# A query bias row and nine gate rows computed by f16 products with the thin matrix standing, on one core

## The chip, the cores and the metric

One core of one Trainium2 chip runs the whole program. The metric is the device time of one execution in microseconds (us), median of several runs. The engines are called PE (TensorE), DVE (VectorE), ACT (ScalarE), POOL (GpSimd) and SP (the queue that issues most DMAs); PEld is PE's loading of the standing operand.

## The reference

x is 8 x 512 tokens of width 512, the context 8 x 120 rows of width 512. A cross-attention layer and an expert layer follow each other:

```
h  = layernorm(x)
kp = ctx @ Wk.T ;  vp = ctx @ Wv.T + bv ;  qp = h @ Wq.T + bq
x1 = x + (softmax(qp @ kp.T / sqrt(512)) @ vp) @ Wo.T + bo
z  = layernorm(x1)
e  = argmax(softmax(z @ Wg + bg))            # one of 8 experts for each token
out = x1 + gelu(z @ W1[e] + b1[e]) @ W2[e] + b2[e]
```

## The kernel before

The kernel has three stages. The first, the preparation, folds weights so that less is left for each token: `kq` is Wk.T @ Wq (key and query weights in one), `ov` is the product of the value and the output weights, and the keys of all eight batches (`J_KEYS`) and their values (`J_VAL`) are made from the context with these. The second stage takes 32 tiles of 128 tokens through attention, picks an expert for each token and writes the rows, sorted by expert, to memory. The third takes 39 tiles of sorted rows through the experts' two layers.

Precision is held by splitting an f32 matrix into a high and a low f16 half (scaled by `WSCALE` = 64) and adding three f16 products of halves; `PARTS` lists the three pairs. So one 512-column f32 result with an inner size of 512 costs four inner blocks x 3 = 12 matmuls. ACT writes the high half and DVE the low half of a result that is split again. ACT, DVE and POOL split the early experts' weights in the same way (`high`, `low`, `split`).

Every product of the preparation is a job with a number. Job n writes PSUM bank n % 8, PE counts finished jobs in `pre_mm`, and ACT and DVE count their copies in `pre_act` and `pre_dve`; `free(n)` makes PE wait until job n - 8 has been copied. The order on each engine is written out by hand and is strict. PE's order is: the products of `kq` (line 1391), the turning of twelve bias rows into columns (line 1399), the column sums of the gate weights (line 1404), the turning of the context (1414) and of Wo (1423), the eight key jobs (1450), the four `ov` jobs (1470), the value bias of the gate (1481, 1484), the value bias (1493), the key bias rows (1503), the eight value jobs (1515) with one turning (1524) among them, and then the token loop, which opens with the turning of x (line 1538).

Two thin results are made beside these. `J_U` is Wk.T @ bq, one number for each of 512 rows: while the second four key jobs run, after each group of three f16 products, `small` adds one f32 product with a 128 x 128 block of Wk standing and one column of the bias moving. `J_WOG` is made in the same places from Wo and the centred gate weights (9 columns). `J_WVG` is Wv times that result (9 columns), one small f32 product after each group of three of the four `ov` jobs. An f32 product is two PE instructions in the trace. Both thin results go to `row_weights` (128 x 4 x 10), are split (lines 850 and 1081) and stand in the key bias products of line 1503.

DVE's order in the preparation: the low halves of Wk and Wq (1036), of `kq` (1022), the copy of the bias columns (1043), the centred gate weights (1049), the split of the value bias (1051, 1053), the low halves of the context and of Wo (1022), the moments of all 32 tiles of x (1027, 1030), the low halves of `ov` (1022), the split of `row_weights` (1081), the copy of the gate's value bias (1085), and then the low halves of the experts' weights (1067) with the copies of the value bias (1091) and the values (1103) among them. SP loads x in groups into four buffers, each refilled when DVE's moments have read it; only behind the sixteen groups come the weights of experts 1 to 3 in its queue, and behind the last moments those of expert 4. The copy of the last value job on DVE also waits for nine pad transfers (`pad_out`), which POOL issues when expert 4 has landed.

Of the kernel before, what the change touches and what calls it, by code (L numbers as in the profile page):

```python
# [5 lines left out]
F16 = mybir.dt.float16  # L6
I32 = mybir.dt.int32
ALU = mybir.AluOpType
# [3 lines left out]
P = 128  # L12
# [128 lines left out]
def build(nc, x, ctx_in, Wk, Wv, bv, Wq, bq, Wo, bo, Wg, bg, W1, b1, W2, b2, out):  # L141
# [6 lines left out]
    with ctx:  # L148
# [22 lines left out]
        key_bias = split_area[0:1 + EM, :]  # L171
        b_stage = bias_area[0:BIAS_ROWS, 0:D]
# [20 lines left out]
        row_weights = sb("row_weights", [P, C, 1 + EM])  # L193
# [142 lines left out]
        rows_split = sem("row_weights_split_parts")  # L336
# [48 lines left out]
        NCONST = 20  # L385
# [23 lines left out]
        J_GSUM = job("dve")  # L409
        J_CTX = job("both", B)  # L410
        J_WOT = job("both", C)
        J_KEYS = job("act", 2 * C)
        J_U = job("act")
        J_WOG = job("act")
        J_OV = job("both", C)
        J_WVG = job("act")
        J_VGB = job("dve")
# [35 lines left out]
        def _(sp):  # L453
# [31 lines left out]
            sp.wait_ge(pre_mm, J_KQ + C)  # L485
# [125 lines left out]
        def _(pool):  # L611
# [10 lines left out]
            nc.gpsimd.memset(bias_rows, 0.0).then_inc(consts, 1)  # L622
            nc.gpsimd.iota(seen[:, 0, :], pattern=[[SPAN // P, E]], base=1, channel_multiplier=0,
# [175 lines left out]
        def _(act):  # L799
# [23 lines left out]
            for k in range(C):  # L823
                n = J_KQ + k
                copy(n, kq[:, 0, k, :], bank[n % 8][:, :], 1.0 / WSCALE)
            for b in range(B):
                n = J_CTX + b
                w = min(P, B * K - P * b)
                copy(n, ctxT[:, 0, :, P * b:P * b + w], bank[n % 8][:, 0:C * w].rearrange("p (c s) -> p c s", c=C))
# [10 lines left out]
            n = J_U  # L840
            copy(n, row_weights[:, :, 0], bank[n % 8][:, 0:C], SCALE)
            n = J_WOG
            copy(n, wo_gate[:, :, :], bank[n % 8][:, 0:C * EM].rearrange("p (c e) -> p c e", c=C))
            for k in range(C):
                n = J_OV + k
                copy(n, ov[:, 0, k, :], bank[n % 8][:, :], 1.0 / WSCALE)
            n = J_WVG
            copy(n, row_weights[:, :, 1:1 + EM], bank[n % 8][:, 0:C * EM].rearrange("p (c e) -> p c e", c=C), 1.0 / WSCALE)
            act.wait_ge(pre_act, copies("act", J_WVG))
            nc.scalar.activation(row_split[:, 0, :, :], row_weights[:, :, :], ACT.Copy, scale=WSCALE).then_inc(rows_split, 1)  # L850
# [155 lines left out]
        def _(dve):  # L1006
# [44 lines left out]
            nc.vector.tensor_scalar(bv_split[:, 0, :], bcol[:, C:2 * C], WSCALE, None, ALU.mult).then_inc(bv_parts, 1)  # L1051
            dve.wait_ge(bv_parts, 1)
# [22 lines left out]
            def ov_low(k):  # L1075
                low_part(J_OV + k, [ov[:, h, k, :] for h in range(2)], bank[(J_OV + k) % 8][:, :], 1.0 / WSCALE)

            for k in range(C):
                ov_low(k)
            dve.wait_ge(rows_split, 1)  # L1080
            nc.vector.scalar_tensor_tensor(row_split[:, 1, :, :], row_weights[:, :, :], WSCALE, row_split[:, 0, :, :],
                                           ALU.mult, ALU.subtract).then_inc(rows_split, 1)
# [288 lines left out]
        def _(pe):  # L1371
# [34 lines left out]

            for b in range(B):
                n = J_CTX + b
                free(n)
                if b in (0, 4, 7):  # L1410
                    pe.wait_ge(ctx_in_at[(0, 4, 7).index(b)], 16)
                w = min(P, B * K - P * b)
                for c in range(C):
                    last = nc.tensor.transpose(bank[n % 8][:, w * c:w * (c + 1)], ctx_nat[0:w, b, P * c:P * (c + 1)],
                                               ident[0:w, 0:w])
                last.then_inc(pre_mm, 1)
# [16 lines left out]
            bq_cols = [bcol[:, e:e + 1] for e in range(C)]  # L1433
# [3 lines left out]
            for h in range(2):  # L1437
                for b in range(4 * h, 4 * h + 4):
                    copied(pe, J_CTX + b)
                if h == 1:  # L1440
                    copied(pe, J_BIAS)
                    copied(pe, J_GSUM)
                    free(J_U)
                    free(J_WOG)
                for c in range(C):
                    n = J_KEYS + C * h + c
                    free(n)
                    for k in range(C):
                        for u, v in PARTS:
                            last = mm(bank[n % 8][:, 0:4 * K], kq[:, u, k, P * c:P * (c + 1)],  # L1450
                                      ctxT[:, v, k, 4 * K * h:4 * K * (h + 1)],
                                      start=(k == 0 and u + v == 0), stop=(k == C - 1 and u == 1))
                        if h == 1:
                            last_u = small(J_U, C * c + k, wk_sb, bq_cols, 1)
                            last_wog = small(J_WOG, C * c + k, wo_sb, wg_cols, EM)
                    last.then_inc(pre_mm, 1)
            last_u.then_inc(pre_mm, 1)
# [5 lines left out]
            free(J_WVG)  # L1463
            wo_cols = [wo_gate[:, e, :] for e in range(C)]
            for k in range(C):
                n = J_OV + k
                free(n)
                for e in range(C):
# [3 lines left out]
                    if k == 0 and e == 0:  # L1472
                        copied(pe, J_WOG)
                    last_wvg = small(J_WVG, C * k + e, wv_sb, wo_cols, EM)
                last.then_inc(pre_mm, 1)
            last_wvg.then_inc(pre_mm, 1)
# [20 lines left out]
            pe.wait_ge(rows_split, 2)  # L1497
# [10 lines left out]
            for k in range(C):  # L1508
                copied(pe, J_OV + k)
# [227 lines left out]
```

## Time and profile before

| | |
|---|---|
| median of 3 runs | 430.65 us (425.63, 430.65, 430.79) |
| profiled execution | 428.8 us, span 427.1 us |
| mean granted TensorE clock | 0.986 |
| busy in the span: PE, DVE, ACT, POOL | 394.9, 321.9, 250.7, 264.7 us |

The span runs from the first to the last instruction of the profiled execution; 1.7 us of its time lie outside. In timelines a row is start, length, engine, line and what was done, with the idle time before it and what ended that in brackets. An engine's busy time says how full it is on average and not what it holds up: that is read from the stretch of the preparation that the change touches.

### The profile page before, as it was taken

Reading aid. Unit: us, or ns where it says so; the run is one execution under the profiler, and the core shown is the slowest. Engines: PE = TensorE matmul, PEld = TensorE weight load, DVE = VectorE, ACT = ScalarE, POOL = GpSimd, SP = SyncE. Lnnn points to the kernel's source line nnn. Section 1 sums busy time; section 2 is a strip of 40 time slices with the busy share of each in tenths; the row PEclk is TensorE's granted clock in tenths of the full one; section 3 lists DMA queues with packets and bytes.
Section 4 is the critical chain, followed back from the end, with each engine's and each line's share of the span. In section 5 each row is a group of like instructions: output and inputs, shape, how many; then the busy total and the mean of one; then the engine's idle time right before and its main releaser. Section 6 shows DMA issues by size and latency. Waiting matters only on the chain.

```text
span 427.1 us, 8876 instructions
## 1 busy us (share of the span) xinstructions
PE 394.9 (92%) x2097; PEld 219.9 (51%) x2097; DVE 321.9 (75%) x658; ACT 250.7 (59%) x571; POOL 264.7 (62%) x338
## 2 busy tenths in 40 slices
PE   7999999979999998997877999999999999999970
PEld 4657774648777676663333444444444444444430
DVE  3499849993678888888687777878779886988640
ACT  5441128768889797865544755555555555656530
POOL 6088960509457777678574375677765665776730
PEclk9999999999999999989998999999999999999997
DMA  8998999908355596465896886988888988898510
GB/s 265 376 400 308 318 424 415 376 21 320 100 162 172 143 352 188 154 187 166 231 274 203 229 246 203 268 255 242 237 246 244 259 252 252 266 267 250 153 51 0
DMA packets 77984, 101.19 MB, mean 237 GB/s; under 512 B 9075, under 2 KB 49023, under 8 KB 76152
## 3 DMA queue, kind: packets, MB, share of 16 engines
q1 hardware_dynamic: 69664, 80.74, 60.8%
q0 software_dynamic: 6400, 19.65, 12.6%
q10 hardware_dynamic: 1880, 0.31, 0.4%
q8 instruction: 19, 0.31, 0.3%
q14 instruction: 21, 0.17, 0.1%
HBM read 70.80 MB, written 31.28 MB: 239 GB/s over the span
## 4 chain that ended last, share of the span: by engine, by line
PE 77%; DVE 10%; issue 4%; DMA 2%; ACT 2%; POOL 2%; SPq 1%; ACTq 0%; DVEq 0%; POOLq 0%
PE bank L1611 27%; PE bank L1614 13%; PE bank L1546 5%; PE bank L1515 5%; PE bank L1450 5%; PE bank L1562 5%; PE bank L1391 3%; PE bank L1538 3%; PE bank L1470 2%; PE bank L1430 2%; PE bank L1548 1%; PE bank L1555 1%; DVE work L1183 1%; PE bank L1503 1%; DVE work L1285 1%
## 5 line engine op out<-in xcount | busy, mean ns | idle before, releaser
L771 POOL DMA_INDIRECT out_x<-keys_values_then_rows_b x39 | 42.9, 1101 | 61.6 <-DVE keys_values_then_rows_b L1296 56.0
L1611 PE MATMUL bank<-expert_weights,ey_bias_split_then_geluT 128*128 x312 | 75.1, 384 | 4.7 <-DVE ey_bias_split_then_geluT L1290 4.7
L1611 PE MATMUL bank<-expert_weights 128*128 x312 | 73.8, 379 | 3.2 <-issue 2.8
L951 ACT ACTIVATE work<-work,b_columns 128x128 f32<-128x128 f32 x148 | 47.3, 390 | 19.8 <-DVE work L1285 11.4
L945 ACT ACTIVATE work<-bank 128x512 f32<-128x512 f32 x37 | 22.1, 596 | 59.7 <-PE bank L1614 45.1
L1611 PEld LDWEIGHTS bank<-expert_weights,ey_bias_split_then_geluT 128*128 128x128 f16 x312 | 30.8, 99 | 42.8 <-issue 8.4
L1611 PEld LDWEIGHTS bank<-expert_weights 128*128 128x128 f16 x312 | 30.5, 98 | 42.0 <-issue 7.7
L1285 DVE STREAM_TRANSPOSE work<-work 128x512 f32<-128x512 f32 x37 | 42.8, 1158 | 12.2 <-DMA work<-hidden_blocks 12.1
L765 POOL TENSOR_TENSOR keys_values_then_rows_b<-keys_values_then_rows_b 128x512 f32<-128x512 f32 x31 | 44.3, 1427 | 8.3 <-POOL keys_values_then_rows_b L757 8.3
L734 POOL DMA_INDIRECT routed_rows<-work,slot_index x32 | 32.4, 1011 | 21.6 <-DVE slot_index L1154 13.8
L1290 DVE TENSOR_TENSOR ey_bias_split_then_geluT<-work,ey_bias_split_then_geluT 128x512 f16<-128x512 f32 x37 | 27.5, 743 | 20.8 <-ACT ey_bias_split_then_geluT L959 19.1
L1614 PE MATMUL bank<-expert_weights 128*128 x156 | 40.0, 379 | 0.0
L1614 PE MATMUL bank<-expert_weights,ey_bias_split_then_geluT 128*128 x156 | 40.0, 379 | 0.0
L757 POOL TENSOR_SCALAR keys_values_then_rows_b<-keys_values_then_rows_b 128x512 f32<-128x512 f32 x39 | 38.2, 982 | 2.5 <-ACT keys_values_then_rows_b L964 0.7
L816 ACT ACTIVATE expert_weights<-expert_weights 128x512 f16<-128x512 f32 x52 | 31.7, 624 | 8.5 <-DVE expert_weights L1067 8.5
L1067 DVE SCALAR_TENSOR_TENSOR expert_weights<-expert_weights 128x512 f16<-128x512 f32 x52 | 34.9, 702 | 1.4 <-ACT expert_weights L816 0.4
L1562 PE MATMUL bank<-keys_values_then_rows_b,work 120*128 120x512 f32 x64 | 35.5, 637 | 0.0
L1546 PE MATMUL bank<-keys_values_then_rows_b,work 128*128 128x128 f32 x256 | 34.7, 280 | 0.0
L1209 DVE TENSOR_TENSOR expert_weights<-key_bias_then_xn,expert_weights 128x512 f16<-128x512 f32 x39 | 31.9, 818 | 1.4 <-ACT expert_weights L937 1.4
L1546 PEld LDWEIGHTS bank<-keys_values_then_rows_b,work 128*128 128x128 f32 x256 | 32.0, 196 | 0.5 <-issue 0.5
L937 ACT ACTIVATE expert_weights<-key_bias_then_xn 128x512 f16<-128x512 f32 x39 | 24.1, 617 | 8.4 <-DVE key_bias_then_xn L1204 8.0
L1296 DVE SCALAR_TENSOR_TENSOR keys_values_then_rows_b<-bank,keys_values_then_rows_b 128x512 f32<-128x512 f32 x39 | 25.7, 658 | 3.1 <-PE bank L1614 3.1
(214 smaller groups left out, 747.5 us busy)
## 6 DMA issues: line engine op xcount, KB each, us to landing
expert_weights<-in_L_ffn_W SPq DMA_DIRECT2D x14, 1024.0 KB, 15.1
keys_values_then_rows_b<-routed_rows SPq DMA_DIRECT2D x39, 258.0 KB, 3.6
hidden_blocks<-work SPq DMA_DIRECT2D x37, 256.0 KB
work<-hidden_blocks SPq DMA_DIRECT2D x37, 256.0 KB
expert_weights<-in_x SPq DMA_DIRECT2D x16, 512.0 KB, 4.8
expert_weights<-in_x SPq DMA_DIRECT2D x24, 256.0 KB, 2.8
work<-routed_rows SPq DMA_DIRECT2D x72, 64.0 KB
key_bias_then_xn<-routed_rows SPq DMA_DIRECT2D x68, 64.0 KB
```

The source lines that it names most:

```text
L734: pool.indirect_dma_start(routed, bass.IndirectOffsetOnAxis(ap=slot_i[:, j:j + 1], axis=0), rows[:, j, :], None).then_inc(sent[j], 16)
L757: x1_again = nc.gpsimd.tensor_scalar(row[:, 0:D], row[:, 0:D], row[:, D + 3:D + 4], row[:, D:D + 1], ALU.mult, ALU.add)
L765: nc.gpsimd.tensor_tensor(row[:, 0:D], row[:, 0:D], kv[:, bass.ds(ex + b2_at, D)], ALU.add).then_inc(res_ready, 1)
L771: pool.indirect_dma_start(out_rows, ids_of, rrow[t.buf][:, 0:D], None, bounds_check=T - 1, oob_is_err=False).then_inc(out_sent[t.buf], 16)
L951: nc.scalar.activation(hid_turned_of(t)[:, P * c:P * (c + 1)], hid_turned_of(t)[:, P * c:P * (c + 1)], ACT.Gelu, bias=b1_cols[:, :, :].rea ...
L1067: nc.vector.scalar_tensor_tensor(w_split[:, bass.ds(n * 2 * D + D, D)], wall[:, bass.ds((n + GAP) * D, D)], WSCALE, w_split[:, bass.ds(n * ...
L1209: nc.vector.tensor_tensor(x2T[t.half][:, C:2 * C, :], xn2_turned.rearrange("p (c t) -> p c t", c=C), x2T[t.half][:, 0:C, :], ALU.subtract) ...
L1285: nc.vector.transpose(hid_turned_of(t).rearrange("p (c j a) -> p a c j", c=C, a=C), hid_in_of(t).rearrange("p (a i c) -> p a c i", a=C, c= ...
L1546: mm(bank[2 + j % 2][:, 0:P], xnT[j % 2][:, c, :], kv[:, bass.ds(b * (2 * D) + c * P, P)], start=(c == 0), stop=False)
L1562: mm(bank[6 + j % 2][:, :], probT[j % 2], kv[0:K, bass.ds(b * (2 * D) + D, D)], start=True, stop=True)\
L1611: mm(o, a[:, c, :], w_split[:, bass.ds(first + (2 * c + h) * D, D)], start=(c == 0 and h == 0 and not begun), stop=False)
L1614: last = mm(o, a[:, C + c, :], w_split[:, bass.ds(first + 2 * c * D, D)], start=False, stop=(c == C - 1))
```

## The change

The two small f32 products are taken out of the key jobs and the `ov` jobs (the one for `J_WOG` stays). In their place stand two jobs of 12 f16 products each, in which the thin matrix is the standing operand and the halves of Wk or Wv move with 512 columns: `J_U` gives one row of 512 numbers, right behind the column sums of the gate weights and ahead of the turning of the context; `J_WVG` gives ten rows (the first is zero), ahead of the last `ov` job. ACT puts the query row over the first of the ten, and a new job `J_RW` turns the ten rows back to columns by four f32 transposes, from which ACT and DVE make the split that `row_weights` gave before. The query bias and `wo_gate` have to be split for this (two operations on DVE for the first; one on ACT and one on DVE for the second, the latter behind the moments of x), and one memset of POOL zeroes the split's first column. SP's loads of experts 1 to 3 wait for `J_U` where they waited for `kq`, since they overwrite the halves of Wk.

```diff
         J_GSUM = job("dve")
+        J_U = job("act")
         J_CTX = job("both", B)
         J_WOT = job("both", C)
         J_KEYS = job("act", 2 * C)
-        J_U = job("act")
         J_WOG = job("act")
-        J_OV = job("both", C)
+        J_OV = [job("both") for _ in range(C - 1)]
         J_WVG = job("act")
+        J_OV.append(job("both"))
+        J_RW = job("both")
...
-            sp.wait_ge(pre_mm, J_KQ + C)
+            sp.wait_ge(pre_mm, J_U + 1)
             for e in range(1, NEARLY - 2):
                 load_expert(e, w_early[e])
...
+            nc.gpsimd.memset(wog_split[:, :, :, :], 0.0).then_inc(consts, 1)
...
# ACT
+            n = J_U
+            act.wait_ge(consts, NCONST)
+            copy(n, u_row, bank[n % 8][0:1, :], SCALE / (WSCALE * WSCALE))
             for b in range(B):
                 n = J_CTX + b
...
-            n = J_U
-            copy(n, row_weights[:, :, 0], bank[n % 8][:, 0:C], SCALE)
             n = J_WOG
             copy(n, wo_gate[:, :, :], bank[n % 8][:, 0:C * EM].rearrange("p (c e) -> p c e", c=C))
+            act.wait_ge(pre_act, copies("act", J_WOG))
+            act.wait_ge(consts, NCONST)
+            nc.scalar.activation(wog_split[:, 0, :, 1:1 + EM], wo_gate[:, :, :], ACT.Copy, scale=WSCALE).then_inc(wog_parts, 1)
...
             n = J_WVG
-            copy(n, row_weights[:, :, 1:1 + EM], bank[n % 8][:, 0:C * EM].rearrange("p (c e) -> p c e", c=C), 1.0 / WSCALE)
-            act.wait_ge(pre_act, copies("act", J_WVG))
-            nc.scalar.activation(row_split[:, 0, :, :], row_weights[:, :, :], ACT.Copy, scale=WSCALE).then_inc(rows_split, 1)
+            act.wait_ge(pre_mm, n + 1)
+            act.wait_ge(pre_act, copies("act", J_OV[C - 2]))
+            nc.scalar.activation(rows_turned, bank[n % 8][0:1 + EM, :], ACT.Copy, scale=1.0 / (WSCALE * WSCALE))\
+                .then_inc(rows_in, 1)
+            act.wait_ge(rows_in, 1)
+            nc.scalar.activation(rows_turned[0:1, :], u_row, ACT.Copy).then_inc(pre_act, 1)
+            n = J_OV[C - 1]
+            copy(n, ov[:, 0, C - 1, :], bank[n % 8][:, :], 1.0 / WSCALE)
+            n = J_RW
+            copy(n, row_split[:, 0, :, :], bank[n % 8][:, 0:C * (1 + EM)].rearrange("p (c e) -> p c e", c=C), WSCALE)
# DVE
             nc.vector.tensor_scalar(bv_split[:, 0, :], bcol[:, C:2 * C], WSCALE, None, ALU.mult).then_inc(bv_parts, 1)
+            nc.vector.tensor_scalar(bq_split[:, 0, :], bcol[:, 0:C], WSCALE, None, ALU.mult).then_inc(bq_parts, 1)
+            dve.wait_ge(bq_parts, 1)
+            nc.vector.scalar_tensor_tensor(bq_split[:, 1, :], bcol[:, 0:C], WSCALE, bq_split[:, 0, :], ALU.mult,
+                                           ALU.subtract).then_inc(bq_parts, 1)
...
+            dve.wait_ge(wog_parts, 1)
+            nc.vector.scalar_tensor_tensor(wog_split[:, 1, :, 1:1 + EM], wo_gate[:, :, :], WSCALE, wog_split[:, 0, :, 1:1 + EM],
+                                           ALU.mult, ALU.subtract).then_inc(wog_parts, 1)
             for k in range(C):
                 ov_low(k)
...
# PE
+            n = J_U
+            pe.wait_ge(bq_parts, 2)
+            for e in range(C):
+                for u, v in PARTS:
+                    last = mm(bank[n % 8][0:1, :], bq_split[:, u, e:e + 1], wk_split[:, v, e, :],
+                              start=(e == 0 and u + v == 0), stop=(e == C - 1 and u == 1))
+            last.then_inc(pre_mm, 1)
...
-                            last_u = small(J_U, C * c + k, wk_sb, bq_cols, 1)
                             last_wog = small(J_WOG, C * c + k, wo_sb, wg_cols, EM)
...
+            def value_gate_rows():
+                n = J_WVG
+                free(n)
+                pe.wait_ge(wog_parts, 2)
+                for e in range(C):
+                    for u, v in PARTS:
+                        last = mm(bank[n % 8][0:1 + EM, :], wog_split[:, u, e, :], wv_split[:, v, e, :],
+                                  start=(e == 0 and u + v == 0), stop=(e == C - 1 and u == 1))
+                last.then_inc(pre_mm, 1)
+
             for k in range(C):
+                if k == C - 1:
+                    value_gate_rows()
...
-                    last_wvg = small(J_WVG, C * k + e, wv_sb, wo_cols, EM)
                 last.then_inc(pre_mm, 1)
-            last_wvg.then_inc(pre_mm, 1)
+
+            n = J_RW
+            free(n)
+            copied(pe, J_WVG)
+            for c in range(C):
+                last = nc.tensor.transpose(bank[n % 8][:, (1 + EM) * c:(1 + EM) * (c + 1)],
+                                           rows_turned[:, P * c:P * (c + 1)], ident[0:1 + EM, 0:1 + EM])
+            last.then_inc(pre_mm, 1)
...
-            pe.wait_ge(rows_split, 2)
+            copied(pe, J_RW)
```

## Rows read from the trace of the kernel before

**Rows 1.** A stretch: length, busy PE, PEld, DVE, ACT, POOL, clock, DMA share

```profile
80.00:90.00 10.00, 10.00 (x53) 6.17 (x51) 9.65 (x15) 5.54 (x11) 0.84 (x1) 1.00 0.60 211
```

**Rows 2.** The chain in order of time: start, length, what set it

```profile
18.67 3.50 PE bank L1414 x32
...
63.67 2.60 PE bank L1493 x12
66.27 4.96 PE bank L1503 x24
...
84.32 0.56 PE bank L1524 x8
84.88 7.91 PE bank L1515 x36
...
94.55 0.64 PE bank L1538 x4
...
101.46 0.96 PE bank L1562 x2
```

**Rows 3.** ACT's copies of a key job without, one with small products, an ov job

```profile
31.39 0.57 ACT L809 ACTIVATE keys_values_then_rows_b<-bank 128x480 f32<-128x480 f32 x1 [1.86 <-PE bank L1450]
...
45.07 0.57 ACT L809 ACTIVATE keys_values_then_rows_b<-bank 128x480 f32<-128x480 f32 x1 [3.30 <-PE bank L1450]
...
58.66 0.60 ACT L809 ACTIVATE expert_weights<-bank 128x512 f16<-128x512 f32 x1 [2.54 <-PE bank L1470]
```

**Rows 4.** Timeline of DVE from the low halves of kq to those of Wo

```profile
17.54 2.48 DVE L1022 SCALAR_TENSOR_TENSOR work<-bank,work 128x512 f16<-128x512 f32 x4 [5.85 <-ACT work L809]
...
20.24 0.16 DVE L1051 TENSOR_SCALAR value_bias_split<-bias_columns 128x4 f16<-128x4 f32 x1
20.43 0.16 DVE L1053 SCALAR_TENSOR_TENSOR value_bias_split<-bias_columns,value_bias_split 128x4 f16<-128x4 f32 x1
20.51 4.60 DVE L1022 SCALAR_TENSOR_TENSOR expert_weights<-bank,expert_weights 128x512 f16<-128x512 f32 x8
25.03 2.47 DVE L1022 SCALAR_TENSOR_TENSOR keys_values_then_rows_b<-bank,keys_values_then_rows_b 128x512 f16<-128x512 f32 x4
```

**Rows 5.** Timeline of DVE from the last moments to the last value's copy

```profile
54.47 0.25 DVE L1030 BATCH_NORM_AGGREGATE mean_var_x<-stats 128x2 f32<-128x6 f32 x2
...
63.70 0.17 DVE L1085 COPY value_gate_bias<-bank 128x9 f32<-128x9 f32 x1 [0.48 <-PE bank L1484]
...
93.77 0.68 DVE L1103 SCALAR_TENSOR_TENSOR keys_values_then_rows_b<-bank,work 120x512 f32<-120x512 f32 x1
```

**Rows 6.** Waits until 100 us, two of DVE's: total us, times, longest

```profile
DVE stats L1027 <- DMA expert_weights<-in_x: 1.8, 3, 0.9
...
DVE expert_weights L1067 <- ACT expert_weights L816: 0.4, 2, 0.2
```

**Rows 7.** SP's issue of the weights of experts 1 to 4, and issue to landing of expert 1's two

```profile
47.57 7.98 SPq L459 DMA_DIRECT2D expert_weights<-in_L_ffn_W  x8
DMA to landing us min/median/max: 8.0/9.6/11.1
```

**Rows 8.** Timeline of ACT and POOL: first split of expert 1, first pad transfers

```profile
62.66 1.13 ACT L816 ACTIVATE expert_weights<-expert_weights 128x512 f16<-128x512 f32 x2
74.52 5.11 POOL L697 DMA_DIRECT2D routed_rows<-keys_values_then_rows_b  x9 [12.09 <-DMA expert_weights<-in_L_ffn_W]
```

**Rows 9.** Windows around idle stretches of PE (columns as in rows 1)

```profile
92.00:96.00 4.00, 1.42 (x8) 0.68 (x7) 3.42 (x6) 3.00 (x7) 0.79 (x1) 1.00 0.04 8
178.00:182.60 4.60, 3.18 (x25) 2.12 (x24) 4.10 (x18) 2.95 (x8) 4.27 (x11) 1.00 0.42 132
182.70:186.10 3.40, 3.40 (x17) 3.06 (x16) 3.26 (x15) 2.21 (x7) 2.26 (x4) 0.50 0.77 195
```

**Rows 10.** Timeline of PE: the same eight score products at either clock

```profile
183.06 1.92 PE L1546 MATMUL bank<-keys_values_then_rows_b,work 128*128 128x128 f32 x8
...
187.26 1.06 PE L1546 MATMUL bank<-keys_values_then_rows_b,work 128*128 128x128 f32 x8
```

## What the change should do

> **What bounds the kernel now.** I read the table of stretches first, then the chain, then the timelines of the two engines that take turns on it. In the preparation PE is busy for the whole of each of the seven stretches of 10 us from 20 to 90 us, of which the last stands in [rows 1]. In the chain every piece from the context's turning at 18.67 on is PE's, one ending where the next begins, until its last value product ends at 84.88 + 7.91 = 92.79 us [rows 2]. So up to there a microsecond of PE's work is a microsecond of time. The end of the stage is DVE's: it copies the last value at 93.77, because it is still splitting expert weights, and is done at 94.45 [rows 5]; the token loop's first transpose starts behind that, at 94.55 [rows 2]. DVE's list, in turn, starts where PE lets it: it stood idle for 0.48 us until the job of line 1484 was done and copied it at 63.70 [rows 5], and from there to the last copy it is packed (9.65 of 10 us busy) [rows 1]. So what counts is by how much PE finishes line 1484 later or earlier. All that follows in the program hangs on the start of the token loop, and I take the shift of that one to one to the end.
>
> **What goes.** ACT copies each key job as it ends, and a copy's length plus the idle time before it is the length of a job: 0.57 + 3.30 = 3.87 us in the second half, 0.57 + 1.86 = 2.43 in the first, which has no small products [rows 3]; the small products cost 1.44 a job, the query bias' and the gate's together. What the one that stays costs is seen in the ov jobs, which have the same shape with one small product a group: 0.60 + 2.54 = 3.14 [rows 3] against 2.60 for twelve f16 products with 512 columns and nothing between (line 1493) [rows 2], so 0.54 a job. The query bias' share is then 1.44 - 0.54 = 0.90, for four jobs 3.6; halving the 1.44 would give 2.9. I take 3.5, near the first, since the row of the remaining shape gives it. In the ov jobs 4 x 0.54 = 2.2 goes. Sum 5.7, bounds 5.1 and 5.8.
>
> **What comes on PE.** Two jobs of 12 products with 512 moving columns. No row has one or ten columns standing and 512 moving; the key bias products have ten standing and 480 moving and take 4.96 / 24 = 0.207 us each [rows 2], which is 0.220 for 512; line 1493 has 128 standing and takes 2.60 / 12 = 0.217. Both say 2.6 us a job, so 5.2 (5.1 to 5.3). The four transposes of ten rows: eight of the same kind took 0.56 [rows 2], so 0.3; the context's, 128 partitions wide, took 3.50 / 32 = 0.11 each [rows 2], which would give 0.44. So PE's work changes by -5.7 + 5.2 + 0.3 = -0.2 us.
>
> By the Trainium skill (TensorE: Matmul & The Clock Gate, LDWEIGHTS) loading 128 standing columns takes 128 / 1.2 = 107 ns whatever the rows, so the 64 f32 loads that go would be worth an estimated 6.8 us, all exposed, and the sum would fall by a further 1.1 us; the rows above, 0.54 us for the four pairs of a job, say that about one load of each pair is hidden, and they decide here.
>
> **The first wait.** PE must have the split query bias before it can start the new row job, and everything that it has is queued behind that: the turning of context and Wo, keys, ov. PE is done with line 1404 at 18.67, where the turning starts [rows 2]. DVE is not: it works on the low halves of kq until 20.02 and writes the value bias' high half at 20.24 [rows 4]. The new operations come there: high half at about 20.35, and the low half one dependent step later (as 20.43 - 20.24 = 0.19) [rows 4], at 20.54, done at 20.70 and seen by PE at some 20.8. In the kernel before, this lag of DVE hid behind 3.5 us of transposes that needed nothing of it. Now PE stands for 20.8 - 18.7 = 2.1 us (1.9 to 2.4), and this is the term that decides the sign.
>
> **The second wait.** The gate rows need the low half of wo_gate, which DVE makes behind all moments of x. The context's copies on DVE now start later by wait and row job: PE's turning begins at 23.4 in place of 18.67, the first copy of ACT is behind the row's copy, and DVE, which started at 20.51 since it was late itself, starts at about 24.6: 4.1 later. Context and Wo take 4.60 + 2.47 (less 0.1 of overlap) as before, so the moments start at 31.5 in place of 27.4, behind the halves of Wo [rows 4], and, if they run as before, end at 54.72 [rows 5] + 4.1 = 58.8; 1.8 us of that was waiting for loads of x [rows 6], which may be less now, so 57.0 to 58.8, and the low half is done by 57.2 to 59.0. PE's last key job ends at 45.07 + 3.87 = 48.94 [rows 3] and ov starts some 0.2 behind, at 49.1; with 2.1 + 2.6 - 3.5 that is 50.3, and wants it three jobs of 2.6 later, at 58.1. So a stall of 0 to 0.9; I take 0.3, since the loads of x find four buffers filled long before and so wait less.
>
> **At nothing.** ACT's copy of the row (a 512-wide copy takes 0.60) [rows 3] delays the context's copies by less than PE's own shift already did, and banks are free in time: the fourth Wo job waits for the copy of the context's fourth block at about 26.9 and starts at 28.4. The two copies of the ten rows lie under the last ov job (1.2 of 2.6 us); without that cover they would cost 1.2. The turned rows are split while PE does 1.8 us of gate bias and 2.6 us of value bias. The memset lies some 10 us ahead of its use. SP passes its new wait long before its queue comes to it: row job done at 23.4, expert 1 issued at 47.57 [rows 7].
>
> **What is moved beside PE.** With the moments 4.1 us later, the groups of x, and behind them experts 1 to 4, are issued up to 4.1 later. Expert 1 is issued at 47.57 and at about 48.1, and lands by about 59.2 [rows 7]; ACT takes it at 62.66 [rows 8], 3.5 later. With 4.1 on one side and the 2.2 below on the other, 1.6 are left. Expert 4 lands at 74.5, the nine pad transfers go out until 79.6 [rows 8], and DVE waits for them only at 93.77 [rows 5]. Both hide.
>
> **Sum.** -0.2 + 2.1 + 0.3 = +2.2 us; bounds +1.2 and +4.1 (-5.8 + 5.1 + 0.3 + 1.9 + 0 = +1.5, less 0.3 if the transposes hide in the last ov job's end; the other ends, -5.1 + 5.3 + 0.44 + 2.4 + 0.9 = +3.9, with 0.2 for semaphores that no row prices). The profiled execution's 428.8 would be 431.0. The median of the three is 430.65, 1.85 above it, and gives 432.9; its runs spread over 5.2 us. I say 432.5.
>
> **Rivals.**
> - *The clock falls in the new wait (+3.8, 434).* The granted clock fell to 0.50, the level of 1.2 GHz, behind a stretch in which PE was idle for 1.4 of 4.6 us, and for 3.4 us [rows 9]. There eight products of line 1546 took 1.92 us where they take 1.06 at 2.4 GHz [rows 10]; half of 3.4 us, 1.6 with the part that was idle anyway, was lost. Against it: PE idled 2.6 of 4 us at the start of the token loop and kept 1.00 [rows 9]. The trace has both, and the new wait is of that size. The Trainium skill (same page, the clock gate) says as much, that an idle TensorE goes back to half its rate.
> - *The loads set the pace (+4.1, 434.8).* If the later loads of x meet more traffic than now, expert 1 lands over 1.6 us later than reckoned, ACT and DVE start their list with it, and the start of the loop moves by the moments' whole 4.1. For it: DVE's moments waited for loads three times already [rows 6]. Against: it is the same traffic with a pause put in.
> - *Not slower (-0.2, 430.4).* DVE's packed list from 63.70 to 94.45 [rows 5] absorbs the shift of PE: PE's last product is done 0.98 us ahead of DVE's copy of it, so DVE, not PE, sets the end, and if it does not start at line 1484's end but could catch up, only PE's work of -0.2 is left. It decides from the point where DVE has idle time to give up; after that it waits 0.4 us in all, for ACT [rows 6], and its order is strict, which speaks against.
> - *Thin standing operands stream slowly (+8.5, over 2%).* If a standing operand of one column fell to the pace of f32 products, with 512 columns in 0.96 / 2 = 0.48 us [rows 2], the 24 products would cost 6.3 more. The ten-column row above speaks against.
>
> **How the numbers follow.** Chances: forecast 0.55, clock 0.18, loads 0.10, not slower 0.13, slow streaming 0.02, and 0.02 for none of these. The range takes in the bounds (-0.2 to +4.1) and the scatter of the runs shown, which is as large: 428.5 to 436. About 2% (8.6 us) is what a measurement of this kernel can tell from no change; only the slow streaming is beyond: faster 0.01, same 0.96, slower 0.03.
>
> **What would show it.** In the profile after: PE idle from 18.7 to about 20.8, released by DVE; twelve products in 2.6 us behind it; second key jobs 2.97 apart; ov jobs 2.6; PE waiting 0 to 0.9 for DVE ahead of the gate rows; the copy of line 1484's result at about 65.9; the token loop's first transpose at about 96.8 in place of 94.55. I am wrong if the token loop starts no later, or if it starts 2 us later and the end does not.

## The result and the profile after

The changed kernel took 434.97 us (median of 4 runs: 432.05, 432.47, 437.47, 439.09), the kernel before 428.14 (4 runs, 424.46 to 430.79): ratio 1.0146, 95% interval 1.0085 to 1.0208, so slower, by 1.5%, with an interval that ends just above 2%. A second, later set gave 434.57 (10 runs) against 432.92 (25 runs), ratio 1.0003 [0.9969, 1.0037]. Ratios leave out executions more than 1.5% above the fastest of their kernel (1 of 4 of the changed kernel in the first set, 4 of 10 in the second, none of the kernel before), medians do not; the profiled execution below, 439.09 us, is one of those left out. Both medians lie inside the forecast range. By its ratio the second set shows no difference, by its medians +1.65 us. So the traces have to carry the explanation.

The page of the changed kernel:

```profile
span 437.4 us, 8814 instructions
...
PE 398.6 (91%) x2061; PEld 215.5 (49%) x2061; DVE 321.1 (73%) x661; ACT 253.0 (58%) x573; POOL 261.0 (60%) x339
```

Its chain, where that of before had nothing but PE from 18.67 us on [rows 2]:

```profile
20.46 0.17 DVE query_bias_split L1073
...
20.68 2.77 PE bank L1437 x12
...
52.15 6.09 DMA expert_weights<-in_x
...
59.93 0.21 DVE wo_gate_split L1102
...
60.27 2.75 PE bank L1498 x12
...
65.72 0.34 PE bank L1517 x4
...
98.82 0.65 PE bank L1581 x4
```

PE's two row jobs (lines 1437 and 1498) are each released by DVE. The second hangs on a load of x of 6.09 us. The token loop starts at 98.82 in place of 94.55. PE's timeline gives the size of the waits, in the brackets:

```profile
17.40 0.23 PE L1425 MATMUL bank<-identity,bias_rows 12*128 12x12 f32 x1
...
20.68 2.75 PE L1437 MATMUL bank<-expert_weights,query_bias_split 128*1 128x512 f16 x12 [2.06 <-DVE query_bias_split L1073]
23.36 3.67 PE L1448 MATMUL bank<-identity,work 128*128 128x128 f32 x32
...
50.39 7.93 PE L1509 MATMUL bank<-keys_values_then_rows_b,work 128*128 128x512 f16 x36
60.27 2.75 PE L1498 MATMUL bank<-work,wo_gate_split 128*10 128x512 f16 x12 [1.95 <-DVE wo_gate_split L1102]
62.95 2.76 PE L1509 MATMUL bank<-keys_values_then_rows_b,work 128*128 128x512 f16 x12
65.65 0.41 PE L1517 MATMUL bank<-identity,ey_bias_split_then_geluT 10*128 10x10 f32 x4
65.99 1.06 PE L1524 MATMUL bank<-wo_gate,bias_columns 128*128 128x9 f32 x8
```

2.06 and 1.95 us of waiting; from start to start the row jobs take 23.36 - 20.68 = 2.68 and 62.95 - 60.27 = 2.68 us, the turning 0.34. ACT's copies answer to [rows 3]:

```profile
47.47 0.57 ACT L817 ACTIVATE keys_values_then_rows_b<-bank 128x480 f32<-128x480 f32 x1 [2.41 <-PE bank L1481]
...
58.36 0.60 ACT L817 ACTIVATE expert_weights<-bank 128x512 f16<-128x512 f32 x1 [1.99 <-PE bank L1509]
```

A second key job is 2.98 long (3.87 before), an ov job 2.59 (3.14). Behind them ACT takes expert 1 without any idle time, so the load had landed:

```profile
66.25 0.20 ACT L817 ACTIVATE row_weights_split<-bank 128x40 f16<-128x40 f32 x1
66.47 1.15 ACT L824 ACTIVATE expert_weights<-expert_weights 128x512 f16<-128x512 f32 x2
```

And DVE:

```profile
31.69 1.27 DVE L1046 BATCH_NORM_STATS2 stats<-expert_weights 128x6 f32<-128x512 f32 x2
...
58.32 1.29 DVE L1046 BATCH_NORM_STATS2 stats<-expert_weights 128x6 f32<-128x512 f32 x2 [1.39 <-DMA expert_weights<-in_x]
59.64 0.25 DVE L1049 BATCH_NORM_AGGREGATE mean_var_x<-stats 128x2 f32<-128x6 f32 x2
...
67.97 0.17 DVE L1111 COPY value_gate_bias<-bank 128x9 f32<-128x9 f32 x1 [0.80 <-PE bank L1527]
```

The moments start at 31.69 and end at 59.89 (before: 27.4 and 54.72) [rows 4, 5].

**Where the 10.3 us between the two spans went.** Executions differ in when the first weights land, so I measure the preparation from PE's turning of the bias rows (17.45 before, 17.40 after) to the token loop's first transpose: 77.10 before, 81.42 after, +4.3. From there to the first expert product the two took 98.6 (193.1 - 94.55) and 99.0 (197.8 - 98.82). The remaining 5.6 us are in the expert stage, 234.0 and 239.6, which the change does not touch; the runs below show how far that stage scatters.

### The profile page after: what moved, and what is told of

Read it like the earlier page. It is cut to its first block, busy times and chain, and to the rows that moved or that the text cites. A ratio compares the mean times of both kernels' runs of the same rounds, so it can differ in the third digit from the quotient of the medians.

```text
span 437.4 us, 8814 instructions
## 1 busy us (share of the span) xinstructions
PE 398.6 (91%) x2061; PEld 215.5 (49%) x2061; DVE 321.1 (73%) x661; ACT 253.0 (58%) x573; POOL 261.0 (60%) x339
## 4 chain that ended last, share of the span: by engine, by line
PE 44%; DVE 19%; DMA 15%; issue 8%; SPq 8%; ACT 3%; POOL 2%; DVEq 0%; ACTq 0%; POOLq 0%
PE bank L1654 11%; DMA work<-hidden_blocks 7%; PE bank L1605 5%; PE bank L1657 5%; PE bank L1558 5%; PE bank L1589 5%; SPq L567 4%; DMA hidden_blocks<-work 4%; DVE stats L1046 3%; DMA expert_weights<-in_x 3%; PE bank L1581 3%; PE bank L1417 3%; DVE expert_weights L1235 2%; DVE key_bias_then_xn L1230 2%; PE bank L1598 1%
## 5 line engine op out<-in xcount | busy, mean ns | idle before, releaser
L779 POOL DMA_INDIRECT out_x<-keys_values_then_rows_b x39 | 41.5, 1065 | 69.0 <-DVE keys_values_then_rows_b L1322 62.5
L1654 PE MATMUL bank<-expert_weights,ey_bias_split_then_geluT 128*128 x312 | 75.5, 386 | 3.4 <-DVE ey_bias_split_then_geluT L1316 3.4
L773 POOL TENSOR_TENSOR keys_values_then_rows_b<-keys_values_then_rows_b 128x512 f32<-128x512 f32 x31 | 41.9, 1353 | 7.7 <-POOL keys_values_then_rows_b L765 7.7
L742 POOL DMA_INDIRECT routed_rows<-work,slot_index x32 | 32.3, 1010 | 20.7 <-DVE slot_index L1180 12.9
L1657 PE MATMUL bank<-expert_weights,ey_bias_split_then_geluT 128*128 x156 | 40.9, 386 | 0.0
L956 ACT ACTIVATE expert_weights<-key_bias_then_xn 128x512 f16<-128x512 f32 x39 | 24.1, 618 | 10.2 <-DVE key_bias_then_xn L1230 9.9
```

What stands on the lines that cost most here:

```text
L742: pool.indirect_dma_start(routed, bass.IndirectOffsetOnAxis(ap=slot_i[:, j:j + 1], axis=0), rows[:, j, :], None).then_inc(sent[j], 16)
L773: nc.gpsimd.tensor_tensor(row[:, 0:D], row[:, 0:D], kv[:, bass.ds(ex + b2_at, D)], ALU.add).then_inc(res_ready, 1)
L779: pool.indirect_dma_start(out_rows, ids_of, rrow[t.buf][:, 0:D], None, bounds_check=T - 1, oob_is_err=False).then_inc(out_sent[t.buf], 16)
L1654: mm(o, a[:, c, :], w_split[:, bass.ds(first + (2 * c + h) * D, D)], start=(c == 0 and h == 0 and not begun), stop=False)
L1657: last = mm(o, a[:, C + c, :], w_split[:, bass.ds(first + 2 * c * D, D)], start=False, stop=(c == C - 1))
```

## The experiments

"Stage" is that distance from the turning of the bias rows to the token loop, 77.1 in the kernel before. "Waits for DVE" are PE's two: ahead of the query bias' row job, then ahead of the gate rows. The fourth column has the start and length of a fall of the clock inside the stage. These columns come from the one profile of each run; the last two are from all executions, the medians in us and the ratio. The first profile's set, e1 to e4, e5 to e8, e9 to e11, and e12 are five sets; a time is compared only with the kernel before in its own set.

| run | stage | waits for DVE | clock at 1.2 GHz in the stage | expert stage | time, before in the same set | ratio, 95% |
|---|---|---|---|---|---|---|
| changed, first profile | 81.4 | 2.06, 1.95 | none | 239.6 | 434.97, 428.14 | 1.0146 [1.0085, 1.0208] |
| e1 | 77.4 | none | none | 233.4 | 432.31, 431.17 | 1.0042 [0.9999, 1.0085] |
| e2 | 81.8 | 2.06, none | 20.7, 6.8 us | 234.9 | 435.43, 431.17 | 1.0081 [1.0038, 1.0124] |
| e3 | 78.1 | none | none | 234.8 | 433.64, 431.17 | 1.0063 [1.0026, 1.0100] |
| e4 | 79.7 | 2.06 | 66.5, 3.4 us | 236.9 | 437.05, 431.17 | 1.0142 [1.0094, 1.0191] |
| e5 | 79.9 | 2.06, 0.81 | none | 236.2 | 434.57, 432.92 | 1.0003 [0.9969, 1.0037] |
| e6 | 83.3 | filled, 2.24 | 61.2, 3.4 us | 234.5 | 437.53, 432.92 | 1.0113 [1.0050, 1.0177] |
| e7 | 82.2 | 2.06 | 20.6, 6.8 us | 237.5 | 434.91, 432.92 | 1.0016 [0.9970, 1.0062] |
| e8 | 77.7 | none | 65.0, 3.4 us | 239.3 | 433.76, 432.92 | 1.0009 [0.9967, 1.0051] |
| e9 | 82.3 | 2.06, none | 20.5, 6.8 us | 237.9 | 434.37, 430.53 | 1.0084 [1.0042, 1.0127] |
| e10 | 81.5 | 2.06, 0.59 | 21.0, 3.4 us | 236.6 | 435.63, 430.53 | one run |
| e11 | 80.6 | filled, 1.58 | none | 236.4 | 433.17, 430.53 | one run |
| e12 | 77.1 | none | none | 236.0 | 433.14, 432.22 | one run |

**e1: the query bias' row job behind the turning of Wo.**

```diff
-        J_U = job("act")
         J_CTX = job("both", B)
         J_WOT = job("both", C)
+        J_U = job("act")
```

(and its products and copy moved alike on PE and ACT).

> The changed kernel with the query bias' row job moved behind the turning of Wo (PE and ACT), nothing else. Theory of the two waits: PE's order of 18.7 us is that of before again, so the wait for the split query bias (2.06) is gone; DVE's moments of x start at 27.4 again and end near 54.7, so the wait for the low half of wo_gate (1.95) goes with it; PE's work is 0.2 more than before. The token loop's first transpose comes at 94.8 (before 94.55, changed kernel 98.82), and the time is within 1 us of before's. Rival, the loads of x set the pace of the preparation: it comes above 97. Rival, the difference in time is the clock's falls, not the preparation: the start moves to 94.8 but the median stays 4 us or more above before's.

PE in its timeline:

```profile
18.81 3.65 PE L1440 MATMUL bank<-identity,work 128*128 128x128 f32 x32
22.39 1.97 PE L1449 MATMUL bank<-identity,expert_weights 128*128 128x128 f32 x16
24.29 2.75 PE L1458 MATMUL bank<-expert_weights,query_bias_split 128*1 128x512 f16 x12
...
56.47 2.76 PE L1499 MATMUL bank<-work,wo_gate_split 128*10 128x512 f16 x12
...
95.11 0.63 PE L1582 MATMUL bank<-identity,work 128*128 128x128 f32 x4 [1.84 <-issue]
```

No bracket at either row job: both waits are gone, and the stage is 77.4 where 77.3 was expected. So both hang on the row job's place ahead of the context. But the second is not a child of the first wait. DVE's moments started at

```profile
27.86 1.27 DVE L1046 BATCH_NORM_STATS2 stats<-expert_weights 128x6 f32<-128x512 f32 x2
```

Counted from the turning of the bias rows they start 10.1 us behind it here and 14.3 in the changed kernel, 4.2 later; PE's first ov product starts 30.9 and 33.0 us behind it (48.61 - 17.74 and 50.39 - 17.40), 2.1 later. The wait stands ahead of both engines' work and moves both; the further 2 us on DVE's side are worked out to be the row job (2.68), which in the changed kernel stands ahead of the blocks that DVE copies, and because of them PE arrives too early. e7, which has the wait (and a fall of the clock) but no row job, agrees: its first ov product moved by 5.0 and its moments by only 3.4. No run has the row job ahead of the context without a wait or a filling.

The time is 1.1 us above before's, with an interval that just reaches no change. The loop did not come above 97, but with the moments early again this order says little of the loads as the pace; e2 does. For the clock see e10.

**e2: the low half of wo_gate ahead of the 14th pair of moments.**

```diff
             for n in range(0, NT // M):
+                if n == 13:
+                    dve.wait_ge(wog_parts, 1)
+                    nc.vector.scalar_tensor_tensor(wog_split[:, 1, :, 1:1 + EM], ...
                 moments_of_x(n)
```

> The changed kernel with DVE's low half of wo_gate put ahead of the 14th of the sixteen pairs of moments instead of behind the last. Theory of the two waits: only the second goes (1.95), the first (2.06) stays; token loop at 96.9, expert 1 having landed in time. Rival, the loads: expert 1, issued at 52.6 in the changed kernel, lands only at 63 to 64 and holds up ACT's and DVE's list; the loop stays at 98 to 98.8.

The stage was 81.8 and not 79.5 (81.42 - 1.95), but not by the loads:

```profile
21.73 5.28 PE L1438 MATMUL bank<-expert_weights,query_bias_split 128*1 128x512 f16 x12 [2.06 <-DVE query_bias_split L1073]
26.94 3.92 PE L1449 MATMUL bank<-identity,work 128*128 128x128 f32 x32
...
62.09 2.75 PE L1499 MATMUL bank<-work,wo_gate_split 128*10 128x512 f16 x12
```

The second wait is gone, expert 1 holds nothing up, and the first wait was followed by a clock of 1.2 GHz: the row job, 2.75 long elsewhere, took 5.28, and the turning 3.92 for 3.67. The windows (length, busy PE, PEld, DVE, ACT, POOL, clock, DMA):

```profile
16.00:20.60 4.60, 3.67 (x21) 2.07 (x19) 2.06 (x4) 2.06 (x4) 0.00 (x0) 1.00 1.05 386
20.70:27.30 6.60, 5.57 (x14) 1.73 (x15) 0.98 (x7) 0.19 (x1) 0.00 (x0) 0.50 1.06 399
```

Less 2.53 + 0.25 it is 79.0, 0.5 below what the theory of the two waits gives; 0.4 of that lies in the idle time ahead of the loop (1.40 us for 1.76).

**e3 and e4: each half of the change alone.** e3 keeps the query bias' small products, e4 the gate's. In outline, against the changed kernel (in both, `row_weights` and its split stay as before):

```diff
# e3
-            n = J_U
+                            last_u = small(J_U, C * c + k, wk_sb, bq_cols, 1)
# e4
-                    value_gate_rows()
+                    last_wvg = small(J_WVG, C * k + e, wv_sb, wo_cols, EM)
```

> Half of the change: the gate's value rows as in the changed kernel, the query bias as small f32 products as before. Two waits: no wait at 18.7, so no late moments, so no second wait either; what is left is work: -2.0 (small products in ov) + 2.7 + 0.35 = +1.05, token loop at 95.6. If the second wait were the gate rows' own and not a consequence of the first, PE would wait some 2 us here too and the loop would start at 97.6.

> The other half: the query bias' row in its place ahead of the context, turned behind the last ov job, the gate's values as small f32 products as before. Two waits: first wait 2.06, work -3.57 + 2.72 + 0.2 for the turning, no second wait as nothing asks for the low half of wo_gate: +1.4, token loop at 95.95. With e3 that makes 2.5 of the changed kernel's 4.27; the remaining 1.8 is the second wait, which needs both halves. Loads theory: the moments are as late as in the changed kernel, so the loop would be at 97.5 or later.

e3: no wait, stage 78.1, +1.0 as expected. The gate rows as such cost a microsecond of PE's work, and the second wait is not theirs alone. The margin was thin: DVE had waited 3.6 us for loads of x, more than in any other profile, and finished the low half at 55.37, 0.14 us ahead of PE's row job.

e4: the first wait is there with 2.06. Up to line 1481's counterpart it is +1.9 (63.62 - 17.44 = 46.2 against 61.73 - 17.45 = 44.3), 0.5 more than its terms gave: 0.15 in the first wait (2.2 from start to start), 0.14 in the turning (0.34 for 0.2), and 0.2 in the ov jobs, most of it at the first group, where the small product waits for the copy of `wo_gate`. Then the clock fell at 66.5, and value bias and key bias took 1.6 longer (4.22 for 2.75, 5.19 for 5.03), but the stage came out at 79.7: only 0.7 of the 1.6 reached the loop, because PE's idle time ahead of it shrank from 1.76 to 0.83 us. So DVE's list absorbs a delay that comes behind line 1484. The moments were as late as in the changed kernel (start 31.63), and the loop was not held to them.

The medians stand in the same order, the first wait's kernels (e2, e4) above those without it (e1, e3), but further apart than the stages. That of e4 is 5.9 above before's where the stage is 2.6 longer, and that of e3 2.5 where it is 1.0; what the rest is, the one profile of each does not show.

**e5, e10, e12: the same kernels again.**

> The changed kernel once more, as the reference of this set of runs. Stage length is read from PE's turning of the bias rows (17.45 before) to the token loop's first transpose (94.55 before): 77.1 before, 81.4 changed. Theory of the two waits alone: the median is 4.3 above before's. With the clock: in some executions it falls in or behind the first wait, as it did in one of the three profiles that have that wait (6.8 us at the lower level, the row job 5.28 in place of 2.75), and the median is 5 to 7 above.

> The changed kernel, one look more at the two waits: the first again 2.06, the second between 0.8 and 2.3 with the waits of DVE for loads of x; whether the clock falls behind the first wait (so far in two of five profiles that have it) is open: stage 80 to 81.5 without, 83 to 84 with.

> The kernel before, one look more. Two waits with the clock: no idle time of PE between 17 and 92 us, no fall of the clock behind 18.7, stage (bias rows to token loop) within 0.3 of 77.1. The token stage, 98.6 from the loop's first transpose to the first expert product, stays within 1.5; the expert stage, 234.0 in the profile of before and 233.4 to 239.6 in the profiles since whatever the edit, may be anywhere in that band: if it is near 234 again, the scatter of that stage would be the edits' after all.

The kernel before had 77.1 a second time (95.26 - 18.15), without a wait or a fall; its token stage took 100.2 us, 0.1 outside the expected band. e5's median is 1.65 us above before's, which meets neither expectation (4.3, or 5 to 7 with the clock). e10's second wait and its stage with a fall both came out smaller than expected (0.59 and 81.5). The changed kernel had its first wait of 2.06 in all three profiles, its second of 1.95, 0.81 and 0.59. In e10 the clock fell behind the first:

```profile
19.76 4.09 PE L1437 MATMUL bank<-expert_weights,query_bias_split 128*1 128x512 f16 x12 [2.06 <-DVE query_bias_split L1073]
...
59.62 2.75 PE L1498 MATMUL bank<-work,wo_gate_split 128*10 128x512 f16 x12 [0.59 <-DVE wo_gate_split L1102]
```

The expert stage took 234.0 and 236.0 in the kernel before, 239.6, 236.2 and 236.6 in the changed one, and 233.4 (e1) and 239.3 (e8) in two kernels whose preparation differs by 0.3 us. So the stage scatters by about the first profile's 5.6 us. Where the scatter arises is not shown. DVE's waits there for `hidden_blocks`, which go through memory, don't follow it (20.0 us in e1, the shortest; 8.3 in e12, 2.6 us longer). Neither does the clock alone: the first profile of the changed kernel spent 10.2 us of the stage at 1.2 GHz and that of before 3.4, but e8 and e12 both spent 6.8. The token stage took 96.8 (e11) to 100.2 us (e2, e12). Whether some part of this follows the edits, these few profiles can't tell.

**e6 and e11: the first wait filled with products whose result is overwritten.**

```diff
             n = J_U
+            for _ in range(9):
+                mm(bank[n % 8][:, :], ones_h[:, :], wk_split[:, 0, 0, :], start=True, stop=True)
             pe.wait_ge(bq_parts, 2)
```

> The changed kernel with nine products of 512 columns, whose result is overwritten, in the place of the first wait (9 x 0.217 = 1.95 us): nothing is computed earlier or later, PE is only not idle. Clock theory: no fall behind 18.7 in any execution, so the median is 1 to 3 us below the changed kernel's in the same set. Waits alone: the same as the changed kernel within 1 us, stage 81.4.

> The changed kernel with the first wait filled, one look more: clock at 2.4 GHz from 16 to 30 us in any case (clock theory); a fall between 18 and 25 us would speak against it. Second wait 0.8 to 2.3.

In both profiles the clock held behind the row job's start, which waits no more (e11):

```profile
20.88 2.75 PE L1439 MATMUL bank<-expert_weights,query_bias_split 128*1 128x512 f16 x12
23.56 3.67 PE L1450 MATMUL bank<-identity,work 128*128 128x128 f32 x32
```

But e6's median did not come down: at 437.53 it is 3 us above the changed kernel's, with an interval that starts above 1. So the expectation of 1 to 3 us less is missed. Its profile has the largest second wait, and now the fall behind that one:

```profile
61.32 4.36 PE L1500 MATMUL bank<-work,wo_gate_split 128*10 128x512 f16 x12 [2.24 <-DVE wo_gate_split L1102]
```

e11 had its second wait of 1.58 without a fall. So the filling took the fall behind the first wait away in these two profiles, and a fall behind the second one remained possible. Why e6's executions are slower than the changed kernel's is open; there were four.

**e7: the wait and nothing else.** The kernel before with the split of the bias and

```diff
+            pe.wait_ge(bq_parts, 2)
             for b in range(B):
                 n = J_CTX + b
```

> The kernel before with the split of the query bias on DVE and PE's wait for it ahead of the context's turning, and nothing else of the change. Waits alone: stage 77.1 + 2.1 = 79.2 and a median 2.1 above before's. Clock theory: the profile shows it at 79.2 or, with a fall, near 80 to 81 (transposes behind it), and the median is 3 to 4 above. If what follows could absorb a shift of the preparation, the median would be under 1 above.

```profile
21.60 6.48 PE L1421 MATMUL bank<-identity,work 128*128 128x128 f32 x32 [2.06 <-DVE query_bias_split L1056]
```

Stage 82.2: 2.06 of wait, and the transposes behind it took 6.48 where they take 3.64, at 1.2 GHz for 6.8 us from 20.6. Without that it is 79.3. The expectation had 80 to 81 with a fall; it was more. The median is 2.0 above before's, where the wait alone was to give 2.1, and the ratio's interval takes in no change. The clock theory's 3 to 4 us are not shown in the time.

**e8: only the query bias' half, behind Wo.** It is e4 with the order of e1.

> Only the query bias' half of the change, its row job behind the turning of Wo. No wait for DVE. Work: 2.72 + 0.34 - 3.57 = -0.5: stage 76.6, the only version below before's 77.1; the median within 1 us of before's, on either side. Rival, thin row jobs cost something that the trace of the preparation does not show (the half with the gate rows alone had a stage of 78.1 but a median 2.5 above before's): the median is 2 above here too.

No wait. Up to the gate bias it is 0.2 us shorter than before (62.41 - 18.35 = 44.06 against 44.28), where -0.5 was expected, with the 0.3 between them in the ov jobs, as in e4. But the clock fell at 65.0 as it did in e4, and the stage was 77.7; of the 1.7 us that the value bias lost (4.44 for 2.75) 0.8 reached the loop. The time is that of before (1.0009 [0.9967, 1.0051]), so the rival of a hidden price of thin rows is not borne out.

**e9: the first pair of moments in DVE's idle time.**

```diff
+            moments_of_x(0)
             for b in range(B):
                 n = J_CTX + b
```

> The changed kernel with the first pair's moments of x moved ahead of the context's low halves, into the 4.07 us in which DVE now stands idle there. One pair (1.6 us) fits if x's first group has landed by 22 us, and SP can issue the fifth group some 9 us earlier. Two waits: the first stays (2.06), the second shrinks from 0.8 to 2.2 (three profiles) to under 0.5, stage 79.4. If the later waits for loads of x set the moments' end, and not their start, the second wait stays above 1 and the stage above 80.5.

```profile
22.36 1.29 DVE L1046 BATCH_NORM_STATS2 stats<-expert_weights 128x6 f32<-128x512 f32 x2 [0.73 <-DMA expert_weights<-in_x]
23.68 0.25 DVE L1049 BATCH_NORM_AGGREGATE mean_var_x<-stats 128x2 f32<-128x6 f32 x2
28.44 4.61 DVE L1041 SCALAR_TENSOR_TENSOR expert_weights<-bank,expert_weights 128x512 f16<-128x512 f32 x8 [4.51 <-ACT expert_weights L817]
```

The pair fits, the second wait is gone, and the first brought a fall of 6.8 us once more (row job 5.28). Less 2.75 the stage is 79.6 (79.4 expected). PE asked for the low half at 61.94 and DVE had it at 61.31: a margin of 0.6 us, of which the early pair gave 1.6; without it DVE would have been 1.0 late. Earlier loads with the moments in their old place were not run.

## Why the prediction was right, and where not

- **What bounds the kernel** held for what comes ahead of line 1484: the changed kernel's shift of the gate bias, 4.3 us, is the stage's. Of delays behind it, in e4 and e8, only about half reached the loop. The two profiles of the kernel before agree to 0.01 us in the stage. That a shift goes one to one to the end of the program is not shown: the token and the expert stage scatter by 3.4 and 6.2 us.
- **The first wait**, the term that decided the sign: 2.1 forecast, 2.06 in every profile that has it (2.2 from start to start).
- **PE's work**: -0.2 forecast, +0.15 found. The second key jobs' four steps gave 3.6 (3.5 forecast), the row jobs took 2.68 each (2.6), the turning 0.34 (0.3); ov gave 2.0 where 2.2 was reckoned, since a bare ov job runs at 2.59 to 2.68. The trace went with the row and not with the 107 ns for each load that the Trainium skill gives (TensorE: Matmul & The Clock Gate, LDWEIGHTS): 64 loads were worth 5.6, not 6.8.
- **The second wait** is the term that was mis-sized: 0.3, at most 0.9, against 1.95, 0.81 and 0.59 in three profiles (2.24 and 1.58 in the two filled ones). The step that was off is "since the loads of x find four buffers filled long before and so wait less". From the first to the last, the moments took 28.2, 27.1 and 26.9 us in the three profiles of the changed kernel (28.5 and 27.8 in the filled ones) against 27.3 and 27.2 in the kernel before: less in two, more in three. DVE empties the four buffers in 6.4 us. From then on each load is issued as its buffer comes free, is needed 3 x 1.6 = 4.8 us later, and took 3.2 to 6.5 us; DVE's waits for loads came to between 0.8 us (e1) and 3.6 (e3) in kernels with the same stream. So the head start is spent after the fourth pair, and one slow load near the end sets the moments' end (in the first profile 6.09 us, with a wait of 1.39): there they started 4.3 later (4.1 forecast) and ended 5.2 later. With loads as in the kernel before, the wait would have been about 1.0, just past the upper bound.
- **The rivals.** *The clock falls in the new wait* had 0.18 and came about in 4 of the 7 profiles with the bare first wait (e2, e7, e9, e10), in neither of the 2 with it filled and in none of the 5 with no wait there (both of before, e1, e3, e8); of the changed kernel's own three profiles it came in one. It cost 1.6 (e10: 4.09 - 2.75 and 0.3) to 2.8 us, so it belonged nearer to one half. *The loads set the pace* is refuted: in the changed kernel, and in e2 without the second wait, ACT took expert 1 as soon as its own list let it. *Not slower* is refuted for the preparation and not for the measured time. *Slow streaming* is refuted: one standing column runs at the pace of 128.
- **The total.** Expected +2.2; the stage showed +4.3, +2.8 and, with a fall, +4.4 in the three profiles of the changed kernel, the time +6.8 in one set and +1.65 in another. The stage's direction is shown by the traces; its +4.3 lies just above the sum's upper bound of 4.1, by the second wait. The size in time is not settled: executions of one kernel scatter by 8 to 9 us, more than the effect. That both medians fell into 428.5 to 436 proves little, since that range also holds no change. The first set's profiled execution owed 5.6 of its 10.3 us to the expert stage. Nor is it shown in time that e1 beats the changed kernel: no set has both.

## What to carry to other kernels

A product that is cheaper by itself can lose on the wait for its operand: ask what the slower engine is doing at the moment when the new consumer comes up, and put the consumer behind work that needs nothing new (e1 undid both waits by an order alone). A new job ahead of the results that another engine works on delays that engine's list by up to its own length, and can make a second wait far behind it: here the 2.68 us of row job came back as 0.6 to 1.95 us at the gate rows. Small products squeezed between big ones are cheap (0.54 us for the four of a job), so taking them out for products of 512 columns wins little: here one of the two halves gained 0.2 us up to the gate bias (e8) and the other lost 1.0 (e3).

## What the runs showed of the hardware

- An idle time of 2.06 us of TensorE was followed by 3.4 or 6.8 us at 1.2 GHz in 4 of 7 profiles. In the changed kernel's first profile, in e2, e7, e9 and e10 the clock also fell once more behind the loop's start, where PE had idled 1.4 to 1.9 us and 0.84, and it did not in the others with the same idle time. The Trainium skill (TensorE: Matmul & The Clock Gate, Why this matters for your kernels) warns of idle gaps between bursts of products as what takes the clock down. The gap that it warns of is longer than this one; here falls followed 2.06 us already, in 4 of 7, and the measurement decides.
- The clock fell with no idle time at all in e4 and e8, behind the last ov job with its small products, four one-row transposes and sixteen small f32 products. Windows of e8:

```profile
61.00:65.00 4.00, 4.00 (x33) 3.27 (x32) 1.43 (x4) 2.04 (x6) 2.91 (x9) 1.00 1.00 420
65.10:68.30 3.20, 3.20 (x9) 1.06 (x7) 3.01 (x6) 2.79 (x5) 0.00 (x0) 0.50 1.03 433
```

PE is busy for all of the four microseconds ahead of the fall. So a PE that the profile shows busy was not safe from it.
- Twelve products of 512 moving columns took 2.68 us with 1, 10 and 128 standing columns.
